# Depthwise convolution taps on ScalarE summed by adding DMAs, and shifted copies in parts of 112 rows

## The reference, cut to what matters

```python
qkv = x @ Wqkv                                   # 8 heads of 16 channels
offsets = [0, 1, 2, 4, ..., 512]                 # each token sees itself and 10 earlier ones
sc = einsum('bhsd,bhskd->bhsk', q, k[pos - offsets]) / sqrt(16)
w = softmax(where(pos >= offsets, sc, -inf))
tele = einsum('bhsk,bhskd->bhsd', w, v[pos - offsets])
conv = depthwise_causal_conv(v, conv_w)          # 7 taps: sum_t conv_w[:, 6 - t] * v[s - t]
fq, fk = elu(q) + 1, elu(k) + 1                  # linear attention over all tokens
low = (fq @ (fk^T v)) / (fq . sum(fk) + 1e-6)
out = x + (tele + conv + low) @ Wo
```

## Time and profile before

| | |
|---|---|
| median of 3 runs | 334.6 us (333.72 to 335.88) |
| the profiled execution's own time | 334.57 us |
| its span in the trace | 332.9 us |
| VectorE busy | 269.8 us, 81% |
| TensorE busy | 253.2 us, 76% |
| ScalarE busy | 176.6 us, 53% |
| GpSimd busy | 72.1 us, 22% |
| moved by DMA | 21.88 MB, mean 66 GB/s |

### The profile page before, as it was taken

How to read it: one execution, slowest core, us unless ns; L and a number is a source line. 1 busy time by engine, 2 the same in 40 slices (tenths; PEclk the granted TensorE clock), 3 DMA queues, 4 the chain that set the end, 5 groups by cost and what they waited for, 6 DMA issues and landing times.

```text
span 332.9 us, 4518 instructions
## 1 busy us (share of the span) xinstructions
PE 253.2 (76%) x1527; PEld 172.3 (52%) x1527; DVE 269.8 (81%) x595; ACT 176.6 (53%) x443; POOL 72.1 (22%) x129
## 2 busy tenths in 40 slices
PE   6668772088589939997898469997797588878894
PEld 6324340087436615776655228767444266675374
DVE  5079996088997999979989999889989989855752
ACT  1683256002536945584769625785478306176851
POOL 4903000001091000302492000221910003131013
PEclk9787979559959987999999959999999569999999
DMA  8200368000024720030038510100248301000003
GB/s 225 70 0 17 99 170 184 26 3 3 4 67 125 213 77 16 0 95 3 19 111 201 156 44 2 32 2 6 78 123 207 103 17 32 0 2 1 1 2 95
DMA packets 20037, 21.88 MB, mean 66 GB/s; under 512 B 3289, under 2 KB 16434, under 8 KB 20014
## 3 DMA queue, kind: packets, MB, share of 16 engines
q1 hardware_dynamic: 20014, 21.59, 23.5%
HBM read 5.07 MB, written 2.10 MB: 22 GB/s over the span
## 4 chain that ended last, share of the span: by engine, by line
PE 32%; DVE 22%; SPq 14%; ACT 12%; DMA 10%; POOL 4%; issue 3%; POOLq 0%; DVEq 0%; ACTq 0%
DMA v_shift<-v_tok 9%; SPq L337 9%; PE psH L1169 7%; PE psA L1089 6%; SPq L336 6%; DVE convT L864 5%; DVE prods L840 3%; PE psY L1266 3%; PE psF L1230 3%; PE psY L1180 2%; POOL rstd L420 2%; ACT xn L576 2%; DVE hid L968 2%; POOL var L418 2%; PE psA L1081 2%
## 5 line engine op out<-in xcount | busy, mean ns | idle before, releaser
L418 POOL TENSOR_SCALAR var<-ss 128x4 f32<-128x4 f32 (+1 forms) x25 | 13.2, 527 | 233.9 <-ACT squares L621 113.6
L260 DVE TENSOR_TENSOR prods<-qT,kT 128x1024 f32<-128x1024 f32 (+1 forms) x44 | 48.8, 1165 | 12.5 <-ACT qT L490 12.5
L1169 PE MATMUL psH<-ident,prods 128*128 128x128 f32 x324 | 42.8, 284 | 0.0
L1169 PEld LDWEIGHTS psH<-ident,prods 128*128 128x128 f32 x324 | 39.0, 148 | 2.3 <-issue 2.3
L420 POOL TENSOR_TENSOR rstd<-var,neg_half 128x4 f32<-128x4 f32 (+2 forms) x29 | 37.8, 1302 | 2.4
L840 DVE TENSOR_TENSOR prods<-v_shift,wgt 128x896 f32<-128x896 f32 x32 | 34.6, 1083 | 0.0
L864 DVE SCALAR_TENSOR_TENSOR convT<-vT,cw,convT 128x1024 f32<-128x1024 f32 x24 | 30.8, 1284 | 0.7
L1137 PE MATMUL psA<-prods,slot_sel 128*32 128x512 f32 x168 | 25.9, 671 | 7.3 <-DVE prods L260 5.3
L840 DVE TENSOR_TENSOR prods<-v_tok,wgt 128x128 f32<-128x128 f32 (+2 forms) x60 | 21.9, 391 | 11.6 <-DMA v_shift<-v_tok 11.6
L1089 PE MATMUL psA<-xnT,wqkv 128*128 128x512 f32 x48 | 28.8, 742 | 3.3 <-ACT xnT L490 3.3
L1230 PE MATMUL psF<-x3T,w 128*128 128x512 f32 x58 | 31.0, 647 | 0.1
(11 more groups left out here) (192 smaller groups left out, 520.3 us busy)
## 6 DMA issues: line engine op xcount, KB each, us to landing
x_in<-L_attn_x SPq DMA_DIRECT2D x4, 512.0 KB, 3.8
x_res<-L_attn_x SPq DMA_DIRECT2D x4, 512.0 KB, 15.6
v_shift<-v_tok SPq DMA_DIRECT2D x4, 508.0 KB
v_shift<-v_tok SPq DMA_DIRECT2D x4, 504.0 KB
v_shift<-v_tok SPq DMA_DIRECT2D x4, 496.0 KB
v_shift<-v_tok SPq DMA_DIRECT2D x4, 480.0 KB
v_shift<-v_tok SPq DMA_DIRECT2D x4, 448.0 KB
out<-y_out SPq DMA_DIRECT2D x7, 256.0 KB, 2.3
```

Of the source, the lines that this page charges most:

```text
L260: return eng.tensor_tensor(prods[:, QUADS * (s % 2) + q, t0:T], qT[:, t0:T], kT[:, PRE - off + t0:PRE - off + T], ALU.mult)
L1169: ins = pe.matmul(dst, terms[:, j % TERM_BUFS, m, :], ident[:], is_transpose=True, start=False, stop=(m == live[-1]))
```

## The change

1. **Shifted copies.** Each main copy is cut at 112 rows: one transfer of 112 rows (or of all, where fewer are left), and for the offsets 1, 2, 4 and 8 one more with the 15, 14, 12 or 8 rows that remain. 18 transfers a batch instead of 14, with the same bytes.
2. **Convolution.** VectorE's `convolve` is gone. ScalarE makes each tap's product by itself (`scale_taps`, a Copy with the tap's column of weights as scale), into seven places (`tap_home`): `convT` (now two, by batch), two new buffers, and `xnT`, `kexp`, `qexp` while they are free. Taps 0 to 3 stand behind `evacuate_v`, ahead of `token_major_v`; tap 4 ahead of `normalise3(2b)`; taps 5 and 6 behind `keep_normed` (in batch 0 taps 4 to 6).
3. **Sums.** GpSimd issues six adding transfers of 512 KB per batch (`add_tap`): 0 += 1 and 2 += 3, then 0 += 4 and 2 += 5, then 0 += 6, then 0 += 2, each waiting for the one before on its side. They stand in GpSimd's list between the layer norms. `add_conv` waits for the last; `features` of the next batch, which overwrites `kexp`, also does.
4. **Softmax in one buffer.** `logit` and `wgt` are dropped; logits and weights are written in place in `prob`. The buffer `squares4` is halved; unit 6 uses `squares`.

```diff
+SHIFT_ROWS = 112
+N_SUMS, N_SIDE = 4, 2
-        convT = sb("convT", [P, T])
+        convT = [sb(f"convT{i}", [P, T]) for i in range(2)]
+        tapT = [sb(f"tapT{i}", [P, T]) for i in range(2)]
+        def tap_home(b, tap):
+            return (convT[b % 2], tapT[0], tapT[1], xnT, kexp, qexp, tapT[0])[tap][:]
@@ shift_v (SyncE)
                 for n, off in enumerate(SHIFTS):
-                    sp.dma_start(v_shift[off:P, n], v_tok[0:P - off]).then_inc(v_shifted, 16)
+                    rows = min(SHIFT_ROWS, P - off)
+                    sp.dma_start(v_shift[off:off + rows, n], v_tok[0:rows]).then_inc(v_shifted, 16)
+                    if off + rows < P:
+                        sp.dma_start(v_shift[off + rows:P, n], v_tok[rows:P - off]).then_inc(v_shifted, 16)
                     sp.dma_start(v_shift[0:off, n, 1:NT], v_tok[P - off:P, 0:NT - 1]).then_inc(v_shifted, 16)
@@ GpSimd
+            def add_tap(b, into, tap, added):
+                nc.gpsimd.dma_start(tap_home(b, into), tap_home(b, tap), accum_op=ALU.add).then_inc(added, N_DMA)
+            def sum_taps_first(b):
+                pool.wait_ge(tap_scaled, upto(b, TAPS, 4))
+                add_tap(b, 0, 1, sums_added)
+                add_tap(b, 2, 3, side_added)
+            def sum_taps_second(b):
+                pool.wait_ge(tap_scaled, upto(b, TAPS, 6))
+                pool.wait_ge(sums_added, N_DMA * upto(b, N_SUMS, 1))
+                add_tap(b, 0, 4, sums_added)
+                pool.wait_ge(side_added, N_DMA * upto(b, N_SIDE, 1))
+                add_tap(b, 2, 5, side_added)
+            def sum_taps_third(b):
+                pool.wait_ge(tap_scaled, upto(b, TAPS, 7))
+                pool.wait_ge(sums_added, N_DMA * upto(b, N_SUMS, 2))
+                add_tap(b, 0, 6, sums_added)
+                pool.wait_ge(sums_added, N_DMA * upto(b, N_SUMS, 3))
+                pool.wait_ge(side_added, N_DMA * upto(b, N_SIDE, 2))
+                add_tap(b, 0, 2, sums_added)
             more_constants()
+            sum_taps_first(0)
...
                     ln4(u0 - 1)
+                if attn:
+                    sum_taps_second(b)
                 if more:
                     ln1(b + 1)
                 if ffn and attn:
                     ln3(u1)
+                if attn:
+                    sum_taps_third(b)
                 if ffn and attn:
                     ln4(u0)
                     add_residual(u0)
                 if attn:
                     ln2(2 * b)
+                if more:
+                    sum_taps_first(b + 1)
                 if attn:
                     ln3(2 * b)
@@ ScalarE
             def evacuate_x(b):
+                if b:
+                    act.wait_ge(side_added, N_DMA * upto(b - 1, N_SIDE, 1))
+            def scale_taps(b, taps):
+                for tap in taps:
+                    if tap == 0:
+                        act.wait_ge(psA_free, freed(b - 1, PSA_V, 1))
+                        if b == 0:
+                            act.wait_ge(conv_ld, 16)
+                            act.wait_ge(consts_ready, 1)
+                        if b >= 2:
+                            act.wait_ge(hT_ready, upto(b - 1, 2, 0))
+                    elif tap == 4:
+                        act.wait_ge(fk_ready, upto(b, 1, 1))
+                    elif tap == 5:
+                        act.wait_ge(fq_ready, upto(b, 1, 1))
+                    elif tap == 6:
+                        act.wait_ge(sums_added, N_DMA * upto(b, N_SUMS, 1))
+                    nc.scalar.activation(tap_home(b, tap), vT[:, VPRE - tap:VPRE - tap + T], ACT.Copy,
+                                         scale=cw[:, TAPS - 1 - tap:TAPS - tap]).then_inc(tap_scaled, 1)
             def features(b):
                 act.wait_ge(psA_free, freed(b - 1, PSA_Q, 1))
+                act.wait_ge(sums_added, N_DMA * upto(b, N_SUMS, 0))
...
                     keep_normed(b)
+                    scale_taps(b, range(5 if b else 4, TAPS))
...
                         evacuate_v(b + 1)
+                        scale_taps(b + 1, range(0, 4))
                     if more:
                         token_major_v(b + 1)
                         token_major_fk(b + 1)
                         norm3_squares(2 * b)
                         norm2(2 * b + 1)
+                        scale_taps(b + 1, range(4, 5))
                         normalise3(2 * b)
@@ VectorE
-                        logit[:, half * TPH:(half + 1) * TPH].rearrange("p j (q s) h -> p (j q) (s h)", s=SLOTS),
+                        prob[:, half * TPH:(half + 1) * TPH].rearrange("p j (q s) h -> p (j q) (s h)", s=SLOTS),
-                softmax_chain(nc.vector.tensor_tensor(wgt[:], prob[:],
+                softmax_chain(nc.vector.tensor_tensor(prob[:], prob[:],
             def add_conv(b, half):
                 dve.wait_ge(terms_summed, upto(b, NT, TPH * (half + 1)))
-                dve.wait_ge(conv_step, upto(b, N_CONV_STEPS, N_CONV_STEPS))
+                dve.wait_ge(sums_added, N_DMA * upto(b, N_SUMS, N_SUMS))
-                    convolve(b, range(0, 3))
                     softmax_logits(b)
-                    convolve(b, range(3, TAPS))
```

More of the change, by code:

```diff
@@ L55 @@
 N_DMA = 16
-N_SHIFT_DMA = 16 * 2 * len(SHIFTS)
+SHIFT_ROWS = 112
+N_SHIFT_DMA = 16 * sum(3 if P - off > SHIFT_ROWS else 2 for off in SHIFTS)
 N_PSA_FULL, N_PSA_FREE = 16, 14
@@ L168, in block_kernel @@
         ss4, var4, rstd4 = sb("ss4", [P, NT]), sb("var4", [P, NT]), sb("rstd4", [P, NT])
-        squares, squares4 = sb("squares", [P, NT, P]), sb("squares4", [P, NT, P])
-        logit = sb("logit", [P, NT, NM, HEADS])
+        squares, squares4 = sb("squares", [P, NT, P]), sb("squares4", [P, TPH, P])
         top = sb("top", [P, NT, HEADS])
@@ L239, in block_kernel @@
         terms_ready, terms_summed = sem("terms_ready"), sem("terms_summed")
-        conv_step, hT_ready, y_ready, yc_ready = sem("conv_step"), sem("hT_ready"), sem("y_ready"), sem("yc_ready")
+        tap_scaled, sums_added, side_added = sem("tap_scaled"), sem("sums_added"), sem("side_added")
+        hT_ready, y_ready, yc_ready = sem("hT_ready"), sem("y_ready"), sem("yc_ready")
         ss2_ready, x2_ready, ss3_ready, xn3_ready = sem("ss2_ready"), sem("x2_ready"), sem("ss3_ready"), sem("xn3_ready")
@@ L550, in exponentials @@
                 act.wait_ge(logit_ready, upto(b, 1, 1))
-                nc.scalar.activation(prob[:], logit[:], ACT.Exp, scale=float(HD) ** -0.5).then_inc(prob_ready, 1)
+                nc.scalar.activation(prob[:], prob[:], ACT.Exp, scale=float(HD) ** -0.5).then_inc(prob_ready, 1)
             def unit_tiles(u):
@@ L614, in norm4 @@
             def norm4(u):
+                kept = squares if u == 2 * B - 2 else squares4
                 if u == 2 * B - 1:
@@ L620, in norm4 @@
                         j = unit_tiles(u)[n]
-                        last = nc.scalar.activation(squares4[:, j, :], output_tile(u, n), ACT.Square,
+                        last = nc.scalar.activation(kept[:, n, :], output_tile(u, n), ACT.Square,
                                                     accum_out=ss4[:, j:j + 1])
@@ L639, in _ @@
             evacuate_v(0)
+            scale_taps(0, range(0, 4))
             for b in range(B + 1):
@@ L804, in softmax_logits @@
                 dve.wait_ge(scores_read, upto(b, 2, 2))
-                softmax_chain(nc.vector.tensor_reduce(top[:], logit[:].rearrange("p j m h -> p j h m"), AX_X, ALU.max))
-                nc.vector.tensor_tensor(logit[:], logit[:], top[:].unsqueeze(2).to_broadcast([P, NT, NM, HEADS]),
+                softmax_chain(nc.vector.tensor_reduce(top[:], prob[:].rearrange("p j m h -> p j h m"), AX_X, ALU.max))
+                nc.vector.tensor_tensor(prob[:], prob[:], top[:].unsqueeze(2).to_broadcast([P, NT, NM, HEADS]),
                                         ALU.subtract).then_inc(logit_ready, 1)
@@ L812, in softmax_weights @@
                 softmax_chain(nc.vector.reciprocal(rden[:], den[:]))
[L813 removed]
+                softmax_chain(nc.vector.tensor_tensor(prob[:], prob[:],
                                                       rden[:].unsqueeze(2).to_broadcast([P, NT, NM, HEADS]),
                                                       ALU.mult))
[L816 removed]
+                softmax_chain(nc.vector.reciprocal(prob[:, :, M_LOW, :], zden[:]))
             def weigh_low(b):
@@ L822, in weigh_low @@
                     tiles = slice(half * TPH, (half + 1) * TPH)
-                    w = wgt[:, tiles, M_LOW, :].unsqueeze(3).to_broadcast([P, TPH, HEADS, HD])
+                    w = prob[:, tiles, M_LOW, :].unsqueeze(3).to_broadcast([P, TPH, HEADS, HD])
                     ins = nc.vector.tensor_tensor(low_terms[:, tiles].rearrange("p j (h d) -> p j h d", d=HD),
@@ L837, in term @@
                 def term(m0, m1, src):
-                    w = wgt[:, j, m0:m1, :].unsqueeze(3).to_broadcast([P, m1 - m0, HEADS, HD])
```

(5 more changed lines are left out.)

4 lines of the change are left out of this document (removed).

## The result

The changed kernel takes 319.83 us (median of 4 runs, 315.91 to 321.26) against 334.21 us; the ratio is 0.952, 95% interval 0.943 to 0.962. Run again beside the experiments, on another chip, it took 318.02 us (ratio 0.950, 0.945 to 0.955). Medians here are over all executions; the ratios leave out those marked slow on record, over 1.5% longer than the fastest of the same kernel. The forecast was 314.0 in a range of 303 to 326. The span of the profiled execution fell from 332.9 to 318.0 us.

The account below looks back on a forecast made before the run. The prediction took VectorE as the bound, alternating with a one-engine `v_shift` transfer in batch 0; gains of 9.6, 1.7, 4.6 and 4.4 us (batches 0 to 3), 20.3 off 334.6, gave 314.3, stated as 314.0, range 303 to 326.

Follow-up runs that it names:

- copies for adds: The changed kernel with its six adding DMAs per batch made plain copies, so the convolution's sum is not computed: 312.3 us, ratio 0.932 to the kernel before.
- batch 0 on VectorE: The changed kernel with batch 0's convolution done by VectorE as before, without scaled taps or adding DMAs there: 312.6 us, ratio 0.930 to the kernel before.

## What to carry over

Before work goes to DMAs, add up all that these engines carry between the start of a needed transfer and its use, with an issue time for each, and count a sum of two tiles in SBUF as two copies. Such adds are free where nothing waits for what they delay (batches 1 to 3, where the engines are as full but `v_shift` has time to spare) and cost their full time where a transfer is awaited (batch 0), so one stage of a loop can want the old form. Count everything that is issued before the awaited transfer lands, a prefetch of the next stage too. When work is taken from the busiest engine, give the next one only what fits its gaps: leaving two of seven taps on VectorE, in the wait that the change had opened there, was worth 5 us.

## What the runs showed of the hardware

- An adding DMA from SBUF to SBUF, 512 KB over 128 rows: 2.85 us of all 16 engines; the same as a copy: 1.46. The share of busy engines shows it, the GB/s doesn't.
- One-engine copies beside adds are far worse than by themselves: SyncE stood 19.77 us in one issue (8.11 before), and the kernel took 384.8 us.
- The same matmuls in batch 2, after the same short waits, stayed at a granted clock of 0.50 for 7 us in both traces of the kernel after, and for 3.5 in two kernels with a shorter batch 0 (copies for adds, batch 0 on VectorE). Why is open.
